# A selective scan on one core: TensorE's order within a pair of steps, and ScalarE's exponential half a step later

## The reference

```
xn    = rms_norm(x) * sigmoid(...)                  # gate from a 512x512 product
delta, B, C = split(xn @ x_proj.T);  dt = softplus(delta @ dt_proj.T + b)
for t in range(1024):                               # the scan
    h = exp(dt[t] * A) * h + (dt[t]*xn[t]) (outer) B[t]     # h: 512 x 128, for each batch row
    y[t] = h . C[t]
x = layer_norm(x + (y + x*D_param) @ out_proj.T)
x = layer_norm(x + (silu(x @ gate.T) * (x @ up.T)) @ down.T)
```

## Time and profile before

| | us |
|---|---|
| median of 3 runs | 2782.92 |
| the profiled execution, its own time | 2790.65 |
| its span, first to last instruction | 2788.8 |
| DVE busy | 2480.8 (89%) |
| PE busy | 2432.3 (87%) |
| ACT busy | 1735.5 (62%) |
| POOL busy | 891.6 (32%) |
| mean granted TensorE clock | 0.972 |

### The profile page before, as it was taken

One profiled execution on the slowest core, in us unless ns is written; L12 is line 12 of the kernel. 1 busy time (PEld: TensorE's weight loads), 2 busy tenths in 40 slices (PEclk: granted clock), 3 DMA queues, 4 the chain that ended last, 5 costly groups with the idle time before them and its releaser, 6 DMA issues.

```text
span 2788.8 us, 51274 instructions
## 1 busy us (share of the span) xinstructions
PE 2432.3 (87%) x17428; PEld 1342.1 (48%) x17428; DVE 2480.8 (89%) x3796; ACT 1735.5 (62%) x2350; POOL 891.6 (32%) x838
## 2 busy tenths in 40 slices
PE   7767679998899988989889898898989988899898
PEld 4322235554455544545445453454535545465557
DVE  6999989998998998999989889899989988988892
ACT  5555366665766666666667757667576655665653
POOL 2343323432334322342223422244223432233320
PEclk8999999999999999999999999999999999999999
DMA  5667666666666765667656675576766656777784
GB/s 168 213 213 235 215 201 199 219 209 219 199 208 209 242 227 156 206 204 248 216 170 219 205 243 195 172 224 216 229 195 199 215 192 208 222 229 236 228 274 158
DMA packets 308275, 588.00 MB, mean 211 GB/s; under 512 B 43370, under 2 KB 59956, under 8 KB 308020
## 3 DMA queue, kind: packets, MB, share of 16 engines
q1 hardware_dynamic: 251828, 449.34, 50.9%
q10 hardware_dynamic: 56192, 135.38, 14.4%
HBM read 565.88 MB, written 18.71 MB: 210 GB/s over the span
## 4 chain that ended last, share of the span: by engine, by line
PE 49%; DVE 19%; issue 15%; ACT 14%; DMA 2%; ACTq 1%; DVEq 0%; SPq 0%
PE banks L1182 18%; PE banks L1435 11%; DVE h L796 11%; PE banks L1348 7%; PE banks L1324 6%; ACT a L1120 5%; DVE banks L774 5%; PE banks L1418 3%; ACT L839 2%; DVE m_sb L774 1%; DVE h L794 1%; DMA U<-in_xT 1%; PE banks L1272 1%; PE banks L1276 1%; ACT L1085 1%
## 5 line engine op out<-in xcount | busy, mean ns | idle before, releaser
L774 DVE TENSOR_TENSOR banks<-a,h 128x512 f32<-128x512 f32 x1670 | 1156.6, 726 | 33.6 <-ACT h L1137 16.5
L1120 ACT ACTIVATE a<-banks 128x2048 f32<-128x2048 f32 x512 | 961.0, 1877 | 268.4 <-PE banks L1348 195.3
L661 POOL TENSOR_TENSOR dexp<-spread,dt 128x512 f32<-128x512 f32 x512 | 538.0, 1051 | 1520.6 <-DVE banks L774 1467.0
L1435 PE MATMUL banks<-h,cz 128*32 128x512 f32 x4096 | 734.1, 621 | 173.4 <-DVE h L796 147.3
L1348 PE MATMUL banks<-dexp,A 32*128 32x256 f32 x8192 | 628.5, 409 | 110.1 <-ACT a L1120 109.8
L796 DVE SCALAR_TENSOR_TENSOR h<-u_bc,BCt,banks 128x512 f32<-128x512 f32 x942 | 696.8, 740 | 0.2 <-PE banks L1435 0.2
L1137 ACT ACTIVATE h<-banks 128x512 f32<-128x512 f32 x378 | 225.9, 598 | 635.4 <-DVE m_sb L774 598.1
L1348 PEld LDWEIGHTS banks<-dexp,A 32*128 32x128 f32 x8192 | 408.0, 190 | 275.6 <-ACT a L1120 208.5
L1182 PE MATMUL banks<-vT,w_ring 128*128 128x256 f32 x1792 | 451.9, 395 | 15.7 <-ACT up L1087 15.2
L774 DVE TENSOR_TENSOR m_sb<-a,banks 128x512 f32<-128x512 f32 x378 | 258.0, 683 | 204.7 <-PE banks L1418 204.4
L1182 PEld LDWEIGHTS banks<-vT,w_ring 128*128 128x128 f32 x1792 | 325.1, 191 | 172.6 <-issue 104.7
(11 more groups left out here) (194 smaller groups left out, 1616.6 us busy)
## 6 DMA issues: line engine op xcount, KB each, us to landing
u_bc<-u_scratch SPq DMA_DIRECT2D x1021, 256.0 KB, 4.0
v_bc<-u_scratch SPq DMA_DIRECT2D x643, 256.0 KB, 4.0
w_ring<-in_gu_w ACTq DMA_DIRECT2D x112, 512.0 KB, 4.9
w_ring<-in_down_w ACTq DMA_DIRECT2D x56, 512.0 KB, 4.6
a<-in_gu_w ACTq DMA_DIRECT2D x16, 512.0 KB, 5.3
x_scratch<-U ACTq DMA_DIRECT2D x21, 384.0 KB, 5.7
x_row<-x_scratch SPq DMA_DIRECT2D x378, 11.2 KB
a<-in_down_w ACTq DMA_DIRECT2D x8, 512.0 KB, 4.8
```

Of the source, the lines that this page charges most:

```text
L661: e.tensor_tensor(dexp[:, q % E_RING, :, :, :], spread[:, :].unsqueeze(1).unsqueeze(1).to_broadcast(shape), by_step[:, :, first:first + BS ...
L774: e.tensor_tensor(dst, a[:, blk % A_RING, b, s, :], src, ALU.mult).then_inc(s_m, 1)
L1120: e.activation(dst.rearrange("p b t (x j) -> p x (b t) j", j=GP), src.rearrange("p g (i r j) -> p (g i) r j", i=PAIR, j=GP), ACT.Exp, scal ...
L1435: last = e.matmul(y_ps[group * GP:(group + 1) * GP, :], cz[:, first:first + GP], h[:, t % H_RING, b * D:(b + 1) * D], start=i == 0, stop=i ...
```

## The change

Two tables and two lines of PE's loop are changed. In the kernel before, PE's order in a pair was: y rows, side work 0, outer product, side work 1, exponents, side work 2 and 3, where these exponents belong to ACT's exponential at the start of the next pair. Now it is: exponents, outer product, y rows, side work 0 to 3. ACT did its exponential at the start of the pair, ahead of side work 0; now it stands between side work 0 and side work 1 of the same pair.

```diff
-EXP_AT = {exp_slot(q): q for q in range(2, TILES_P)}
-P_AT = {exp_slot(q) - (2 if exp_slot(q) > 2 * (q - 2) else 0): q for q in range(2, TILES_P)}
+EXP_AT = {exp_slot(q) + (1 if exp_slot(q) > 2 * (q - 2) else 0): q for q in range(2, TILES_P)}
+P_AT = {exp_slot(q): q for q in range(2, TILES_P)}
@@ tensor(e), the loop over steps
                     if SLOTS * t + i in P_AT:
                         exponents(P_AT[SLOTS * t + i], p_ps)
+                    if i == 0 and t in on_x:
+                        add_inputs(t)
                     if i == 0 and t % 2 == 0 and t:
                         y_row(t - 2)
                         y_row(t - 1)
-                    if i and t in on_x:
-                        add_inputs(t)
                     for stage, x, j in plans[c].get(SLOTS * (t % TB) + i, ()):
```

## The result

The changed kernel took 2855.86 us (median of 4 runs, 2848.68 to 2858.58) against 2785.14 us of the kernel before on the same chip (4 runs, 2780.05 to 2792.65): a ratio of 1.0246, 95% interval 1.022 to 1.0273. It is slower, as forecast: by 71 us between the medians, and by 63.6 us between the two profiled executions (span 2852.4 against 2788.8), where 47 were forecast.

What follows compares the result with a forecast made beforehand. DVE and PE, both near nine tenths busy, were taken as the bound, PE having as little to spare. Chunks 1 to 6 +32, chunk 0 0, chunk 7 +15: +47 us, against the median 2782.92 giving 2830, range 2772 to 2885.

Steps and rivals of the forecast that it cites:

- what would show it: Signs expected in the changed trace: outer product wait near 204 us, state copy above 16.5, PE behind L1087 50 to 100.
- The sum for chunk 2: Over its 64 pairs, new DVE waits of 30.5 us against 25.2 that go: +5.3 us per chunk.
- four cycles of three pairs: Feed forward block: three pairs take 16.4 us, PE-bound with a 1.6 us wait for the `act`; 7.4 us per chunk.
- behind the first layer norm, gates and selections: Group after the layer norm, gates and selections following each other through the one bank: 6.2 us of new DVE waits.
- end of the gate and up stage: Pairs with `act`, output projection and two `utc`, ACT in half step 1 and PE in 2: 4.6 us.
- transfers: ACT piece starting six transfers: the state copy behind it comes 1.88 us later, on top of 1.45; 3.3 us.
- behind the second softplus: The pair behind the second softplus, late on both orders: 3.5 us of new DVE waits.
- single pairs: Five pairs, most following one with two side pieces, PE's 6.2 us against DVE's 4.5: about 1.1 each, 5.5 us.
- rival A: Faster, chance 0.18: outer product nearly free ahead of y rows, single pairs absorb lateness, only ACT's waits stay; 2736 us.
- The gain of 25.2 us: Chunk 2: DVE's stops caused by y rows and side work ahead of the outer product all go, if nothing is late next.
- Chunk 7: Last chunk: five pairs go from 26.7 to 29.9 us, three such cycles +9, later `act` pieces about 6: +15 us.
- C: Rival, much slower, chance 0.18: state copy behind the late exponential; ten more pairs per chunk pay 0.9 us each; 2893 us.

Runs made afterwards that it cites:

- experiment 1: The kernel before with only the outer product moved ahead of the y rows, exponents and ACT's exponential at their old places: 2779.37 us, ratio 0.9976.
- experiment 5: The changed kernel with ACT's exponential one half step later still, behind half step 1, PE's order as changed: 2729.63 us, ratio 0.9789 to the kernel before.

## Why the prediction was right, and where its sizes were off

**Direction and mechanism: right.** Most items of what would show it are there: fewer waits for the outer product (111, not 164); the state copy's wait far above 16.5 us; PE behind L1087 with 91.1 us in 52 stops, 1.61 us in the row above for 1.6 forecast; outer product to y rows 0.31 for 0.3; the pair behind the layer norm 1.9 us longer for 1.8. Two items missed: the wait for the outer product is 147.0 us, not near 204, since part of what I put there stands at the state copy; and the y rows' wait on DVE is down from 147.3 to 39.2 us, not gone. The cause is shown and not only argued: the same PE order with the exponential elsewhere gives 2913, 2856, 2730 and 2769 us, and half an exponential takes 119 us off.

**The sum for chunk 2**, forecast 30.5 us of DVE's waits, measured 18.2 + 15.7 = 33.9 between 702 and 1044 us:

```profile
DVE m_sb L774 <- PE banks L1418: 18.2, 13, 5.0
DVE banks L774 <- ACT h L1137: 15.7, 14, 3.2
```

| term, us | forecast | measured |
|---|---|---|
| four cycles of three pairs | 7.4 | 5.4 |
| behind the first layer norm, gates and selections | 6.2 | 10.8 |
| end of the gate and up stage | 4.6 | 3.0 |
| transfers | 3.3 | 3.2 |
| behind the second softplus | 3.5 | 5.0 |
| single pairs | 5.5 | 2.3 |
| behind the second layer norm, and the pair after | 0 | 4.3 |

- *The cycle* was forecast at 16.4, measured at 16.0. (Four times the forecast 1.8 are 7.2, not 7.4.) I had PE's need as the bound of all three pairs; the stop of 0.9 to 1.0 us is at the state copy behind the `act`, which one pair pays; another pays 0.4 us for the outer product, and the third nothing.
- *Gates and selections* are the term that was mis-sized most, by 4.6 us in chunk 2. Two things were not in it. I carried the lateness forward on PE only, and in the changed kernel's timeline the gate and its table load stand on ScalarE behind the exponential, with the state copy behind them (1.70 us), and the next exponents are late for it too. The other is TensorE's clock, below.

```profile
754.09 1.88 ACT L1120 ACTIVATE a<-banks 128x2048 f32<-128x2048 f32 x1 [1.83 <-PE banks L1348]
755.99 1.28 ACT L869 ACT_TABLE_LOAD   x1
757.28 1.02 ACT L869 ACTIVATE dt<-banks,half_gate_bias,half_gate 128x256 f32<-128x256 f32 x2
758.20 0.59 ACT L1137 ACTIVATE h<-banks 128x512 f32<-128x512 f32 x1
...
758.89 0.70 DVE L774 TENSOR_TENSOR banks<-a,h 128x512 f32<-128x512 f32 x1 [1.70 <-ACT h L1137]
...
763.31 0.69 DVE L774 TENSOR_TENSOR m_sb<-a,banks 128x512 f32<-128x512 f32 x1 [2.33 <-PE banks L1418]
```

- *The second layer norm* was put at nothing, though the earlier trace rows had priced the first one: 4.3 us in chunk 2, 1.8 of them in its own pair and 2.4 in the pair after.
- *Single pairs* were forecast as late by PE's need of 6.2 against 4.5; most absorbed it. Here rival A was right about the slack.
- *The gain of 25.2 us* if nothing is late next did not come alone either: experiment 1, which has no late exponential, keeps 209 of 221 us.

**The term that was left out: TensorE's clock.** The changed kernel's PE behind the first layer norm, and the granted clock (PEclk, third from the end) of part of it:

```profile
741.10 1.41 PE L1348 MATMUL banks<-dexp,A 32*128 32x256 f32 x16 [3.73 <-ACT a L1120]
742.31 0.63 PE L1418 MATMUL banks<-x_row 9*128 9x512 bf16 x1
742.87 1.93 PE L1435 MATMUL banks<-h,cz 128*32 128x512 f32 x8
744.97 3.78 PE L1182 MATMUL banks<-U,w_sel 128*128 128x256 f32 x8 [0.17 <-ACT vT L1074]
748.68 1.15 PE L1348 MATMUL banks<-dexp,A 32*128 32x256 f32 x16
```

```profile
742.00:748.00 6.00, 5.83 (x24) 2.72 (x17) 4.59 (x7) 2.85 (x3) 0.61 (x2) 0.50 0.40 125
```

PE had stood idle for 3.73 us, waiting for the exponential, and then worked at 0.50, which is 1.2 GHz in place of 2.4: this selection piece takes 748.68 - 744.97 = 3.71 us, a `gu` of the same shape 1.92. In chunk 2 it happens at three more places: at the second selection (758.36, after 3.13 us idle, 3.20 us), behind the second softplus (902.16, after 3.25 us, 3.61 us) and behind the second layer norm (705.59, after 5.75 us, exponents to outer product 1.88 us for 0.97). By these differences about 6 of the 33.9 us are the clock, an estimate, and nearly 4 of them are in the gates and selections; none of DVE's waits of the kernel before in chunk 2 came behind such a stretch. Such a stop of PE is thus paid twice, and the forecast had it once.

Over the chunks the forecast was nearer than its terms, and by luck: the clock and the second layer norm were missing, and the cycle, the end of gate and up and the single pairs were too large. Chunks 1 to 6 grew by 3.8, 10.5, 3.2, 5.1, 13.1 and 2.7 us, together by 38.4 for 32. Chunk 2, from which the forecast was made, grew by twice its 5.3. The granted clock of the chunks shows why they differ:

| chunk | 1 | 2 | 3 | 4 | 5 | 6 |
|---|---|---|---|---|---|---|
| before, us | 335.9 | 331.3 | 338.1 | 335.3 | 332.7 | 344.4 |
| before, granted clock | 0.98 | 0.99 | 0.97 | 0.98 | 0.98 | 0.96 |
| changed, us | 339.7 | 341.8 | 341.3 | 340.4 | 345.8 | 347.1 |
| changed, granted clock | 0.96 | 0.97 | 0.96 | 0.96 | 0.95 | 0.94 |

Chunks 2 and 5, which grew most, were the shortest before, and chunk 2 had the highest clock. Within a plan that is the same, one pair of the cycle takes 5.9 us in chunk 2 at a clock of 1.00 and 7.5 in chunk 3 at 0.77. (The plan is the same in chunks 1 to 5 only; that of chunk 6 differs from its 77th step on.) The clock is part of the size and not a rival for the cause: over chunks 1 to 6 the changed kernel, experiment 1 and experiment 5 all have a granted clock of 0.96 and take 2056, 2001 and 1942 us.

Chunk 0 is unchanged (322.3 and 322.1), as forecast. Chunk 7 grew by 21.9 for 15: its five pairs of the earlier trace rows came as forecast (29.2 us, once 30.9, for 29.9), the rest is mostly in state copies behind pieces in half step 2 and the layer norm. With the 3.4 us of start and tail these are the 17 us between 47 and 63.6. So the mechanism held and its sizes did not: behind the long pieces of ScalarE and at the gates the terms were too small, partly for want of the clock, and those for the cycle, the end of gate and up and the single pairs too large.

**The rivals.** Experiment 5 takes 2730 us and A had 2736, but not by A's way, and the nearness is luck: the outer product is not nearly free there, it costs the same 0.30 us, and what went are the waits behind the exponential that A had kept. Of A, its slack in the single pairs was right. C was the other half of the truth: the state copy does pay, 119.2 us in 104 places, but mostly in place of the outer product's wait, so the total is two fifths of the way from the forecast to C. Both could have been told apart beforehand by asking of each pair which of the two waits ends last, which I did for PE and not for ScalarE.

**What stays open**: 3 us of the span, how much of the 63.6 us the clock makes over all chunks, and why a stop of 1.6 us in the cycle leaves the clock at 1.00 in chunk 2 and not in chunk 3. The mean granted clock, 0.948 here and 0.972 before, does not order the times: experiment 5 has 0.951 and is 2% faster than before.

## What to carry to other kernels

Where three engines work a pair of steps in program order, moving one producer (here the exponents) is worth what its consumer's queue makes of it: ask what stands behind the consumer, and who waits for that. The biggest wait in the profile names the instruction that ended last, not the gain; with the outer product early, 73 of 85 us came back at the next wait in line. A stop also has a second price where the clock falls behind it. And a half step in one table (2856 to 2730 us) was worth more than the whole change (71 us), so sweep the consumer's place before judging the producer's.

## What the runs showed of the hardware

A 9 row bf16 matmul of 512 columns takes 0.22 us to another of its kind, 0.30 to 0.31 to the y rows, and about 0.1 with the 32 row exponents, all at full clock; to the y rows at a granted clock of 0.5 it takes 0.56. The neighbour sets the price. The Trainium skill ("TensorE: Matmul & The Clock Gate", section "Back-to-back issue gap") gives 216 ns for an isolated matmul of 512 columns: the trace agrees for the same kind in a row and not ahead of the y rows. An ACT table load is 1.28 us ahead of the gates, and it sits in ScalarE's queue like any other piece. An engine's average misleads here: ScalarE is busy only 61% in the changed kernel (about a tenth of idle time, as said ahead of the prediction, holds for DVE and PE alone), and it is what the other two wait for. And behind a stop of 3.1 to 5.8 us TensorE's granted clock was 0.5, at which the same selection or gate piece took 3.2 to 3.7 us for 1.92.
